# Local attention with normalised probabilities: GpSimd multiplies them by reciprocal sums before TensorE turns them

## The chip, the core and the metric

The kernel runs on one core of one Trainium2 chip, as one program for a whole network. The metric is device time in microseconds (us), the median of the runs. A profiled execution gives a trace of every instruction on the core's engines: TensorE (PE, its weight loads PEld), VectorE (DVE), ScalarE (ACT), GpSimd (POOL) and SyncE (SP), which here only issues transfers.

## The reference

The network has four blocks on 8 sequences of 256 tokens with 128 features. The part that matters here stands in two places: a transformer of six layers whose attention is local. Each layer projects a token row to queries, keys and values of 16 heads of 64, normalises and rotates queries and keys, and attends in windows of 32 tokens, each query to its own window and the one before:

```python
sim = jnp.einsum('bhwie,bhwje->bhwij', bq, bk2) * QK_SCALE
sim = jnp.where(mask, -jnp.finfo(sim.dtype).max, sim)
attn = jax.nn.softmax(sim, -1)
out = jnp.einsum('bhwij,bhwje->bhwie', attn, bv2)
...
out = out.transpose(0, 2, 1, 3).reshape(b, n, INNER)
return out @ Wo
```

A gated feed-forward with a layer norm follows in each layer. The two transformers begin their first full turns at some 641 and 3011 us of the span.

## The kernel before

A turn is one sequence in one layer: 6 layers times 8 sequences are 48 turns for each transformer, 96 in all. The 16 heads of a turn are 8 pairs, and the turn has 8 slots p = 0 to 7, one for a pair. All engines walk through the same slots, each with its own list of calls written out by hand (`pe_window`, `act_window`, `dve_window`, and the loop of GpSimd over `pool_spread` and `pool_prepare`). Engines run in order; semaphores counted up by one tie them together. The lists are skewed: in slot p the scores belong to pair p + 2, and between them lie pieces of the projection and rotation of the next turn (T + 1), and of the feed-forward of the turn two before (T - 2).

A pair goes this way. TensorE makes the scores of pair p + 2 in slot p (`pe_scores`, L1716), two heads in PSUM banks 0 and 1, 128 queries by 128 or 160 keys for the two halves of the sequence. VectorE adds the mask, scales, copies to `pairs` and takes the negated maximum (`dve_negmax`, L2090). ScalarE computes the exponentials in place and their sums (`act_probs`, L1983) a slot later. VectorE takes the reciprocals of the four columns of sums at the start of slot p (`dve_recip`, L2099). TensorE turns the exponentials (four transposes to bank 2, `pe_turn_probs`, L1728 and L1729) first thing in slot p, and ScalarE copies them to `pairsT` (`act_copy_probs`, L1990). VectorE turns the 32x32 blocks of the previous window that the four transposes leave out (`dve_turn_prev`, L2110). In slot p + 1 TensorE multiplies with the values to bank 4 or 5 (`pe_weigh`, L1750).

The division by the sums comes after that product. GpSimd spreads the reciprocals over 64 columns per head (`pool_spread`, L1944), TensorE turns them to the second half of bank 4 or 5 (`pe_shares`, L1738), ScalarE copies this to `shares` (`act_copy_shares`, L1995), and VectorE multiplies context by shares into `ctxT` (`dve_share`, L2104). After all 8 pairs TensorE multiplies by Wo (`pe_out`, L1819), in slot 6 of the next turn.

What else stands in the slots: TensorE makes two projection chunks of the next turn in each of the slots 0 to 5 (`pe_chunks`, L1784) into banks 6 and 7, each of which waits until its bank has been read. ScalarE copies them in the slot behind (`act_copy_chunk`): a query or key chunk needs a square (L2003) and a copy (L2007), a value chunk one copy (L2010), so slots 1, 2, 4 and 5 have four such operations and slots 3 and 6 two. ScalarE's list for a slot begins with these copies. VectorE sums the squares and makes the sine part (`dve_rotate`, L2121 and L2129), GpSimd the cosine part and the sum (L1960, L1967) and scales the keys (L1973). In slots 2 and 6 VectorE works out inverse roots in twelve small steps (`dve_roots`, L2145 to L2151), in slot 2 behind the statistics of the feed-forward (`dve_ff_stats`, L2161 to L2166).

Of the kernel before, what the change touches and what calls it, by code (L numbers as in the profile page):

```python
# [12 lines left out]
ALU = mybir.AluOpType  # L13
# [1613 lines left out]
def windowed_transformers(nc, sem, c, name, io):  # L1627
# [7 lines left out]
             "probs_ready", "probsT_in_psum", "probsT_ready", "prev_ready", "recip_ready", "spread_ready", "ctx_in_psum", "shares_ready", "ctx_ready",  # L1635
# [8 lines left out]
     s.probs_ready, s.probsT_in_psum, s.probsT_ready, s.prev_ready, s.recip_ready, s.spread_ready, s.ctx_in_psum, s.shares_ready, s.ctx_ready,  # L1644
# [51 lines left out]
    def run(number):  # L1696
        T0, T1 = number * TURNS, (number + 1) * TURNS

        def has_turn(turn):
            return T0 <= turn < T1  # L1700
# [20 lines left out]
        def pe_turn_probs(pe, T, p):  # L1721
            pe.wait_ge(s.probs_ready, T * PAIRS + p + 1)
# [9 lines left out]
        def pe_shares(pe, T, p):  # L1732
            pe.wait_ge(s.spread_ready, T * PAIRS + p + 1)
            if T * PAIRS + p - 1 > T0 * PAIRS:

                pe.wait_ge(s.ctx_ready, T * PAIRS + p - 1)
            for t in range(HALVES):
                pe.transpose(c.bank[4 + p % 2][:, S + t * P:S + (t + 1) * P], c.spread[:, p % 2, t * P:(t + 1) * P],  # L1738
                             c.ident[:, :])

        def pe_weigh(pe, T, p):
            pe.wait_ge(s.probsT_ready, T * PAIRS + p + 1)
            pe.wait_ge(s.prev_ready, T * PAIRS + p + 1)
# [143 lines left out]
        def pe_window(pe, T):  # L1887
            following = has_turn(T + 1)
            for p in range(PAIRS):
                pe_turn_probs(pe, T, p)  # L1890
                if p >= 1:
                    pe_shares(pe, T, p - 1)
                elif has_turn(T - 1):
                    pe_shares(pe, T - 1, PAIRS - 1)
# [24 lines left out]
                if p == 5 and has_turn(T - 2):  # L1919
                    pe_turn_normed(pe, T - 2)  # L1920

        def pe_tail(pe):
            L = T1 - 1
            pe_shares(pe, L, PAIRS - 1)
# [14 lines left out]
        def pool_spread(g, T, p):  # L1939
            g.wait_ge(s.recip_ready, T * PAIRS + p + 1)  # L1940
            if T * PAIRS + p - 2 >= T0 * PAIRS:

                g.wait_ge(s.ctx_in_psum, T * PAIRS + p - 1)
            g.tensor_copy(c.spread[:, p % 2, :].rearrange("p (n d) -> p n d", n=4),  # L1944
                          c.recip[:, 0, 4 * (p % 4):4 * (p % 4) + 4].unsqueeze(2).broadcast_to((P, 4, DH))
                          ).then_inc(s.spread_ready, 1)
# [46 lines left out]
        def act_copy_shares(a, T, p):  # L1993
# [531 lines left out]
```

## Time and profile before

| | |
|---|---|
| median of 3 runs | 6058.27 us (6057.07 to 6066.74) |
| the profiled execution: span from first to last instruction | 6062.1 us |
| busy share of the span: PE, DVE, ACT, POOL | 89%, 70%, 65%, 45% |
| one turn in the middle of a transformer | 44.64 us |
| granted TensorE clock, mean over the span | 0.947 |

The profiled execution's own time is its span; it is not timed besides. The busy share counts the time in which an engine runs at least one instruction; matmuls are pipelined, so it is not a share of peak. In the rows below, the order of time on an engine gives the start, the duration, the engine, the line, the operation, its output and inputs and how often it stands there in a row; in brackets stands how long the engine had been idle before it, and what released it. Neighbouring instructions of an engine can overlap in their records by some 0.1 us; the distance between starts is the time that each takes of the queue.

### The profile page before, as it was taken

How to read it: one execution, taken by the hardware profiler on the slowest of the kernel's cores; microseconds unless marked ns; L12 is line 12 of the kernel's file. 1: busy time of each engine (PE TensorE's matmuls, PEld its weight loads, DVE VectorE, ACT ScalarE, POOL GpSimd, SP SyncE). 2: the span in 40 equal slices, each digit the busy share in tenths (PEclk: the TensorE clock that was granted, in tenths of full speed). 3: DMA queues.
4: the chain of work that ended last, by engine and by line, in shares of the span. 5: the costliest groups of instructions: out<-in, count | busy, mean ns of one | idle time of the engine just before them, and what ended most of it. 6: DMA issues, size and time to landing. Idle time of an engine off the chain costs nothing. (4 is left out here: it accounts for less than half of the span.)

```text
span 6062.1 us, 121575 instructions
## 1 busy us (share of the span) xinstructions
PE 5372.5 (89%) x41154; PEld 3794.5 (63%) x41154; DVE 4241.2 (70%) x16112; ACT 3913.4 (65%) x11510; POOL 2700.1 (45%) x2578
## 2 busy tenths in 40 slices
PE   7885699999999999997489999999999999697989
PEld 5674366666666666665256666666666666464678
DVE  4453688888888888885378888788888887454522
ACT  2211588888888888884178888888888888222333
POOL 0000556556565565652166656566565665230000
PEclk9996799999999999998599999999999999697999
DMA  0000000000000000000000000000000000000000
GB/s 11 22 1 3 22 1 12 9 12 9 1 15 6 12 9 12 8 1 4 21 1 7 10 6 12 9 12 9 4 13 6 12 8 1 5 2 4 2 29 8
DMA packets 30964, 53.45 MB, mean 9 GB/s; under 512 B 7688, under 2 KB 17168, under 8 KB 29712
## 3 DMA queue, kind: packets, MB, share of 16 engines
q1 hardware_dynamic: 30352, 45.66, 2.4%
q8 instruction: 339, 5.55, 0.4%
q14 instruction: 273, 2.24, 0.1%
HBM read 44.60 MB, written 1.05 MB: 8 GB/s over the span
## 5 line engine op out<-in xcount | busy, mean ns | idle before, releaser
L1784 PE MATMUL bank<-wA,next_rowT 128*128 128x512 f32 x2304 | 1213.7, 629 | 194.6 <-DVE turnB L2129 73.1
L1983 ACT ACTIVATE pairs<-pairs,negmax 128x128 f32<-128x128 f32 (+1 forms) x3072 | 1236.8, 418 | 18.6 <-DVE negmax L2090 17.5
L1960 POOL TENSOR_TENSOR turnA<-raw,ropes 128x512 f32<-128x512 f32 x768 | 968.7, 1271 | 169.3 <-ACT raw L2007 140.4
L2090 DVE CUSTOM_DVE_ANT_0 pairs<-bank,bands,big 128x128 f32<-128x128 f32 (+1 forms) x3072 | 941.7, 364 | 64.6 <-PE bank L1716 61.0
L1967 POOL TENSOR_TENSOR qk<-turnA,turnB 128x512 f32<-128x512 f32 x768 | 975.8, 1271 | 0.0
L1944 POOL COPY spread<-recip 128x256 f32<-128x256 f32 x768 | 305.3, 398 | 1257.8 <-DVE recip L2099 1251.4
L1784 PEld LDWEIGHTS bank<-wA,next_rowT 128*128 128x128 f32 x2304 | 369.6, 190 | 676.7 <-DVE turnB L2129 294.3
L1990 ACT ACTIVATE pairsT<-bank 128x512 f32<-128x512 f32 x768 | 465.9, 607 | 302.2 <-PE bank L1729 301.9
L1983 ACT ACTIVATION_READ_ACCUMULATOR pairs<-pairs,negmax 128x1 f32 x3072 | 625.0, 203 | 0.0
L285 POOL TENSOR_TENSOR rstd<-vareps,neg_half 128x2 f32<-128x2 f32 x56 | 39.0, 696 | 1292.4 <-DVE vareps L256 892.7
L2129 DVE TENSOR_TENSOR turnB<-bank,ropes 128x512 f32<-128x512 f32 x768 | 523.1, 681 | 0.0
L1973 POOL TENSOR_TENSOR qk<-qk,big 128x1024 f32<-128x1024 f32 x192 | 365.7, 1905 | 341.3 <-DVE recip L2204 327.9
L1807 PE MATMUL bank<-ident,qk 128*128 128x128 f32 x3072 | 431.1, 279 | 41.5 <-ACT big L2010 16.4
L2007 ACT ACTIVATE raw<-bank 128x512 f32<-128x512 f32 x768 | 461.1, 600 | 0.0
L1807 PEld LDWEIGHTS bank<-ident,qk 128*128 128x128 f32 x3072 | 344.7, 142 | 156.1 <-issue 131.6
L1728 PE MATMUL bank<-ident,pairs 128*128 128x128 f32 x1536 | 383.4, 277 | 27.7 <-ACT pairs L1983 27.7
L1729 PE MATMUL bank<-ident,pairs 128*128 128x128 f32 x1536 | 377.7, 273 | 0.0
L1819 PEld LDWEIGHTS bank<-wB,ctxT 128*128 128x128 f32 x3072 | 357.8, 192 | 8.4 <-issue 0.3
L1819 PE MATMUL bank<-wB,ctxT 128*128 128x128 f32 x3072 | 358.8, 275 | 0.0
L1728 PEld LDWEIGHTS bank<-ident,pairs 128*128 128x128 f32 x1536 | 216.1, 141 | 178.3 <-ACT pairs L1983 90.8
L2104 DVE TENSOR_TENSOR ctxT<-bank,shares 128x256 f32<-128x256 f32 x768 | 306.1, 399 | 8.6
L1850 PE MATMUL bank<-xT,wC 128*128 128x256 f32 (+1 forms) x1152 | 305.4, 402 | 6.9 <-ACT big L2038 3.7
(306 smaller groups left out, 11272.8 us busy)
## 6 DMA issues: line engine op xcount, KB each, us to landing
wA<-in_wt_wqkv SPq DMA_DIRECT2D x72, 256.0 KB, 2.8
wB<-in_wt_wo SPq DMA_DIRECT2D x12, 512.0 KB, 3.5
wC<-in_wt_w SPq DMA_DIRECT2D x12, 341.0 KB, 2.9
wD<-in_wt_w SPq DMA_DIRECT2D x12, 192.0 KB, 2.4
big<-in_e_up SPq DMA_DIRECT2D x1, 2048.0 KB
big<-in_e_down SPq DMA_DIRECT2D x1, 2048.0 KB
scl<-in_wt_scales SPq DMA_DIRECT2D x12, 128.0 KB, 3.1
X<-in_x SPq DMA_DIRECT2D x8, 128.0 KB, 2.5
```

The lines of the kernel that those rows point to most:

```text
L1728: pe.transpose(out[:, 0:P], probs[:, 0:P], c.ident[:, :])
L1729: last = pe.transpose(out[:, P:2 * P], probs[:, P + WINDOW:2 * P + WINDOW], c.ident[:, :])
L1784: pe.matmul(side_bank(i)[:, :], c.next_rowT[:, t * P:(t + 1) * P], wqkv[:, k * 512:(k + 1) * 512], start=True, stop=True).then_inc(s.chunk ...
L1807: done = pe.transpose(side_bank(i)[:, (2 * k + t) * P:(2 * k + t + 1) * P], c.qk[:, t, which, at:at + P], c.ident[:, :])
L1819: done = pe.matmul(c.bank[6][:, t * D:(t + 1) * D], ctxT[T % 2][:, k, t * P:(t + 1) * P], wo[:, k * D:(k + 1) * D], start=(k == 0), stop=( ...
L1960: g.tensor_tensor(c.turnA[:, m % 2, :].rearrange("p (h d) -> p h d", h=8), c.raw[:, m % 4, :].rearrange("p (h d) -> p h d", h=8), cos, ALU ...
L1967: g.tensor_tensor(c.qk[:, t, k // 2, (k % 2) * 512:(k % 2) * 512 + 512], c.turnA[:, m % 2, :], c.turnB[:, m % 4, :], ALU.add).then_inc(s.s ...
L1983: last = a.activation(tile, tile, ACT.Exp, scale=-1.0, bias=c.negmax[:, 2 * p + side, t:t + 1], accum_out=c.pair_sums[:, p % 4, t, side:si ...
L1990: a.activation(whole_blocks(c.pairsT[:, 2 * (p % 2):2 * (p % 2) + 2, :]), c.bank[2][:, :].rearrange("p (n k) -> p n k", n=4), ACT.Identity ...
L2007: last = a.activation(c.raw[:, m % 4, :], src, ACT.Identity)
L2090: last = v.tensor_tensor_reduce(c.pairs[:, 2 * (p % 4) + side, AT[t]:AT[t] + SPAN[t]], c.bank[side][:, AT[t]:AT[t] + SPAN[t]], c.bands[:, ...
L2129: v.tensor_tensor(out, turned, sin.unsqueeze(1).broadcast_to((P, 8, 2, DH // 2)), ALU.mult).then_inc(s.chunk_rotated, 1)
```

## The change

The exponentials are multiplied by the reciprocal sums before they are turned, in place in `pairs`, by GpSimd (`pool_shares`, two multiplies for a pair, one for each half). So the product with the values gives the normalised context at once, and ScalarE copies it from PSUM to `ctxT` (`act_copy_ctx`). `pe_shares`, `pool_spread`, `act_copy_shares` and `dve_share` go. `pe_turn_probs` moves from the start to the end of TensorE's slot and waits for GpSimd; `act_copy_probs` moves by one slot, to the same place in the next slot's list; `dve_turn_prev` moves to the end of VectorE's slot and waits for GpSimd too.

```diff
         def pe_turn_probs(pe, T, p):
-            pe.wait_ge(s.probs_ready, T * PAIRS + p + 1)
+            pe.wait_ge(s.shares_ready, T * PAIRS + p + 1)
...
-        def pe_shares(pe, T, p):
-            pe.wait_ge(s.spread_ready, T * PAIRS + p + 1)
-            if T * PAIRS + p - 1 > T0 * PAIRS:
-
-                pe.wait_ge(s.ctx_ready, T * PAIRS + p - 1)
-            for t in range(HALVES):
-                pe.transpose(c.bank[4 + p % 2][:, S + t * P:S + (t + 1) * P], c.spread[:, p % 2, t * P:(t + 1) * P],
-                             c.ident[:, :])
-
         def pe_weigh(pe, T, p):
             pe.wait_ge(s.probsT_ready, T * PAIRS + p + 1)
             pe.wait_ge(s.prev_ready, T * PAIRS + p + 1)
+            if T * PAIRS + p - 1 > T0 * PAIRS:
+
+                pe.wait_ge(s.ctx_ready, T * PAIRS + p - 1)
...
         def pe_window(pe, T):
             following = has_turn(T + 1)
             for p in range(PAIRS):
-                pe_turn_probs(pe, T, p)
-                if p >= 1:
-                    pe_shares(pe, T, p - 1)
-                elif has_turn(T - 1):
-                    pe_shares(pe, T - 1, PAIRS - 1)
                 if p + 2 < PAIRS:
                     pe_scores(pe, T, p + 2)
...
                 if p == 5 and has_turn(T - 2):
                     pe_turn_normed(pe, T - 2)
+                pe_turn_probs(pe, T, p)
...
-        def pool_spread(g, T, p):
+        def pool_shares(g, T, p):
             g.wait_ge(s.recip_ready, T * PAIRS + p + 1)
-            if T * PAIRS + p - 2 >= T0 * PAIRS:
-
-                g.wait_ge(s.ctx_in_psum, T * PAIRS + p - 1)
-            g.tensor_copy(c.spread[:, p % 2, :].rearrange("p (n d) -> p n d", n=4),
-                          c.recip[:, 0, 4 * (p % 4):4 * (p % 4) + 4].unsqueeze(2).broadcast_to((P, 4, DH))
-                          ).then_inc(s.spread_ready, 1)
+            for t in range(HALVES):
+                probs = c.pairs[:, 2 * (p % 4):2 * (p % 4) + 2, AT[t]:AT[t] + SPAN[t]]
+                at = 4 * (p % 4) + 2 * t
+                last = g.tensor_tensor(probs, probs, c.recip[:, 0, at:at + 2].unsqueeze(2).broadcast_to((P, 2, SPAN[t])),
+                                       ALU.mult)
+            last.then_inc(s.shares_ready, 1)
...
-        def act_copy_shares(a, T, p):
+        def act_copy_ctx(a, T, p):
             a.wait_ge(s.ctx_in_psum, T * PAIRS + p + 1)
-            a.activation(c.shares[:, p % 2, :], c.bank[4 + p % 2][:, S:2 * S], ACT.Identity).then_inc(s.shares_ready, 1)
+            a.activation(ctxT[T % 2][:, p, :], c.bank[4 + p % 2][:, 0:S], ACT.Identity).then_inc(s.ctx_ready, 1)
...
-                act_copy_probs(a, T, p)
+                if p >= 1:
+                    act_copy_probs(a, T, p - 1)
+                elif has_turn(T - 1):
+                    act_copy_probs(a, T - 1, PAIRS - 1)
...
-        def dve_share(v, T, p):
+        def dve_turn_prev(v, T, p):
+
             v.wait_ge(s.shares_ready, T * PAIRS + p + 1)
-            v.tensor_tensor(ctxT[T % 2][:, p, :], c.bank[4 + p % 2][:, 0:S], c.shares[:, p % 2, :],
-                            ALU.mult).then_inc(s.ctx_ready, 1)
-
-        def dve_turn_prev(v, T, p):
-
-            v.wait_ge(s.probs_ready, T * PAIRS + p + 1)
+            if T * PAIRS + p - 1 > T0 * PAIRS:
+                v.wait_ge(s.ctx_in_psum, T * PAIRS + p - 1)
...
                 dve_recip(v, T, p)
-                if p >= 2:
-                    dve_share(v, T, p - 2)
-                elif has_turn(T - 1):
-                    dve_share(v, T - 1, p + PAIRS - 2)
-                dve_turn_prev(v, T, p)
                 if p == 7 and has_turn(T - 2):
                     dve_last_hidden(v, T - 2)
...
                     if has_turn(T + 2) and starts_layer(T + 2):
                         dve_tables(v, T + 2)
+                dve_turn_prev(v, T, p)
...
                     for p in range(PAIRS):
-                        pool_spread(g, T, p)
+                        pool_shares(g, T, p)
```

## Rows read from the trace of the kernel before

**Rows 1.** Busy time by stretch (one turn; a later stage), and the next row's transposes.

```profile
2015.03:2059.67 44.64, 42.31 (x305) 29.43 (x303) 36.54 (x146) 36.86 (x113) 26.66 (x26) 1.00 0.13 37
5100.00:5400.00 300.00, 240.60 (x2366) 164.52 (x2366) 156.50 (x501) 103.88 (x262) 97.73 (x46) 0.83 0.01 3
...
L1765 PE MATMUL bank<-ident,Y x192: 272/328/473, 641.2 to 5098.2; 128*128 128x128 f32 x192
```

**Rows 2.** Order of time on TensorE over one turn.

```profile
2015.40 0.71 PE L1750 MATMUL bank<-pairsT,big 128*64 128x160 f32 x8
...
2019.27 0.27 PE L1728 MATMUL bank<-ident,pairs 128*128 128x128 f32 x1
...
2019.70 0.38 PE L1738 MATMUL bank<-ident,spread 128*128 128x128 f32 x2
2020.02 0.77 PE L1716 MATMUL bank<-kT,qT 64*128 64x128 f32 x8
2020.71 0.71 PE L1750 MATMUL bank<-pairsT,V 128*64 128x160 f32 x8
...
2022.80 1.88 PE L1784 MATMUL bank<-wA,next_rowT 128*128 128x512 f32 x4
...
2025.96 0.71 PE L1750 MATMUL bank<-pairsT,V 128*64 128x160 f32 x8
...
2027.76 1.94 PE L1784 MATMUL bank<-wA,next_rowT 128*128 128x512 f32 x4
...
2030.98 0.71 PE L1750 MATMUL bank<-pairsT,V 128*64 128x160 f32 x8
...
2032.96 1.13 PE L1784 MATMUL bank<-wA,next_rowT 128*128 128x512 f32 x2 [0.25 <-ACT qT L2015]
...
2036.89 0.71 PE L1750 MATMUL bank<-pairsT,V 128*64 128x160 f32 x8
...
2041.21 0.71 PE L1750 MATMUL bank<-pairsT,V 128*64 128x160 f32 x8
...
2047.82 0.71 PE L1750 MATMUL bank<-pairsT,V 128*64 128x160 f32 x8
...
2053.86 0.27 PE L1728 MATMUL bank<-ident,pairs 128*128 128x128 f32 x1
...
2055.31 0.71 PE L1750 MATMUL bank<-pairsT,V 128*64 128x160 f32 x8
...
2060.03 0.71 PE L1750 MATMUL bank<-pairsT,V 128*64 128x160 f32 x8
```

**Rows 3.** Order of time on ScalarE, slot 1 and the start of slot 2.

```profile
2019.08 0.58 ACT L2003 ACTIVATE sq<-bank 128x512 f32<-128x512 f32 x1
...
2020.99 0.62 ACT L1990 ACTIVATE pairsT<-bank 128x512 f32<-128x512 f32 x1
...
2023.86 0.60 ACT L2003 ACTIVATE big<-bank 128x512 f32<-128x512 f32 x1 [0.40 <-PE bank L1784]
```

**Rows 4.** Order of time, VectorE and GpSimd in slot 2; all instances of L2166.

```profile
2028.89 1.27 POOL L1967 TENSOR_TENSOR qk<-turnA,turnB 128x512 f32<-128x512 f32 x1
2028.95 1.24 DVE L2166 TENSOR_SCALAR big<-big 128x2 f32<-128x2 f32 x1
...
2030.22 0.18 DVE L2145 TENSOR_SCALAR big<-big 128x34 f32<-128x34 f32 x1
...
2033.04 0.39 DVE L2104 TENSOR_TENSOR ctxT<-bank,shares 128x256 f32<-128x256 f32 x1
...
L2166 DVE TENSOR_SCALAR big<-big x96: 170/1246/1259, 779.2 to 5193.1; 128x2 f32<-128x2 f32 x96
```

**Rows 5.** Groups of instructions by line on GpSimd.

```profile
L1967 POOL TENSOR_TENSOR qk<-turnA,turnB 128x512 f32<-128x512 f32 x768 | 975.8, 1271 | 0.0
...
L1973 POOL TENSOR_TENSOR qk<-qk,big 128x1024 f32<-128x1024 f32 x192 | 365.7, 1905 | 341.3 <-DVE recip L2204 327.9
...
L1944 POOL COPY spread<-recip 128x256 f32<-128x256 f32 x768 | 305.3, 398 | 1257.8 <-DVE recip L2099 1251.4
```

More of the change, by code:

```diff
@@ L1634, in windowed_transformers @@
              "qT_in_psum", "kT_in_psum", "qT_copied", "kT_copied", "scores_ready", "scores_seen", "negmax_ready",
-             "probs_ready", "probsT_in_psum", "probsT_ready", "prev_ready", "recip_ready", "spread_ready", "ctx_in_psum", "shares_ready", "ctx_ready",
+             "probs_ready", "probsT_in_psum", "probsT_ready", "prev_ready", "recip_ready", "shares_ready", "ctx_in_psum", "ctx_ready",
              "out_in_psum", "shifted_in_psum", "normed", "normedT_in_psum", "normedT_ready",
@@ L1643, in windowed_transformers @@
      s.qT_in_psum, s.kT_in_psum, s.qT_copied, s.kT_copied, s.scores_ready, s.scores_seen, s.negmax_ready,
-     s.probs_ready, s.probsT_in_psum, s.probsT_ready, s.prev_ready, s.recip_ready, s.spread_ready, s.ctx_in_psum, s.shares_ready, s.ctx_ready,
+     s.probs_ready, s.probsT_in_psum, s.probsT_ready, s.prev_ready, s.recip_ready, s.shares_ready, s.ctx_in_psum, s.ctx_ready,
      s.out_in_psum, s.shifted_in_psum, s.normed, s.normedT_in_psum, s.normedT_ready,
@@ L1920, in pe_window @@
                     pe_turn_normed(pe, T - 2)
+                pe_turn_probs(pe, T, p)
         def pe_tail(pe):
             L = T1 - 1
-            pe_shares(pe, L, PAIRS - 1)
             pe_weigh(pe, L, PAIRS - 1)
@@ L2062, in act_window @@
                 if p >= 1:
-                    act_copy_shares(a, T, p - 1)
+                    act_copy_ctx(a, T, p - 1)
                 elif has_turn(T - 1):
-                    act_copy_shares(a, T - 1, PAIRS - 1)
+                    act_copy_ctx(a, T - 1, PAIRS - 1)
                 if has_turn(T - 2):
@@ L2073, in act_tail @@
             L = T1 - 1
-            act_copy_shares(a, L, PAIRS - 1)
+            act_copy_probs(a, L, PAIRS - 1)
+            act_copy_ctx(a, L, PAIRS - 1)
             for f in (L - 1, L):
@@ L2256, in dve_tail @@
             L = T1 - 1
-            dve_share(v, L, PAIRS - 2)
-            dve_share(v, L, PAIRS - 1)
             dve_ff_add(v, L - 2)
```

## Prediction

> **What bounds the kernel now.** I read the busy-time view of one turn first [rows 1]. One turn of the local attention takes 44.64 us. TensorE is busy for 42.31 of them, ScalarE for 36.86, VectorE for 36.54 and GpSimd for 26.66, at a granted clock of 1.00. There are 96 such turns in two stages; the transposes of the next row (L1765), two of each turn, run from 641.2 to 5098.2 [rows 1], and 85 of the 94 distances between turns inside a stage lie within 0.02 us of 44.64. So nearly all of both stages is one pattern, and what a turn wins or loses counts some 92 times (the first three turns and the last of each stage differ). The order of time on TensorE [rows 2] then shows a queue with hardly a hole: the eight "weigh" groups of a turn (L1750; I call them W0 to W7 by the slot in which they run) have their successors close behind. TensorE sets the turn, with VectorE just behind it. ScalarE and GpSimd are free enough only as long as nobody waits for them at once. ScalarE's order of time [rows 3] shows how late it is inside a slot: in slot 1 it copies the turned probabilities (L1990) at 2020.99, after four copies of projection chunks and after TensorE has begun the weigh group at 2020.71.
>
> **What the change removes.** Two transposes of the spread sums per slot on TensorE (L1738): from their start to that of the scores 0.32 us pass (2019.70 to 2020.02, [rows 2]); over 768 slots that is at most 246 us. By the pitch of the four transposes before them (0.43 us for four, 2019.27 to 2019.70) it is at least 165 us. On VectorE a product of 0.39 us per slot goes (L2104, [rows 4]). On ScalarE one 128x256 copy takes another's place and costs nothing new. On GpSimd a copy of 398 ns goes [rows 5].
>
> **What it adds.** Two in-place GpSimd multiplies per slot, of 256 and 320 elements a partition. No row has this shape. The nearest is L1973, in place with a broadcast factor as here: 1905 ns for 1024 elements [rows 5]. In proportion 576 elements are 1.07 us: the low end. A line through it and L1967 (1271 ns for 512) has 0.64 us fixed per instruction and gives 0.95 + 1.03 = 1.99 us: the high end. L1967's own rate, 2.48 ns an element, gives 1.43. I take 1.4 us, 1.0 us more than the copy that goes, since it lies between the two. GpSimd's turn becomes 26.7 + 8.0 = 34.7 us, which is no bound by its sum; it would be one from some 2.9 us a pair on.
>
> **What it moves.** Three things that were half a slot or more early now sit on a loop. (a) The probabilities of a pair are turned at the slot's end, their ScalarE copy comes a slot later, behind the chunk copies, and the weigh group stands only the scores (0.69 us, 2020.02 to 2020.71) behind the transposes. (b) VectorE's turn of the previous window's part (L2110) goes to the very end of its slot. In slot 2 that is behind the feed-forward statistics and the inverse roots, and the weigh group of slot 3 waits for it. (c) The transposes wait for GpSimd. Behind a waiting weigh group stands all of TensorE's later work, the next chunks first, and behind these stand ScalarE's copies and VectorE's rotations.
>
> **The new turn, worked out.** Zero is the start of W0, at 2015.40. Before, W1 to W7 and the next W0 start at 5.31, 10.56, 15.58, 21.49, 25.81, 32.42, 39.91 and 44.63 [rows 2].
>
> W1: ScalarE starts the chunk copies at 3.68 as before (2019.08, [rows 3]); four copies take 1.91 (to 2020.99), the probabilities' copy 0.62 and the semaphore 0.07: 6.28. TensorE, its scores done at 5.0, waits 1.3 us.
>
> W2: W1 to the next chunks is 2.09 (2020.71 to 2022.80, [rows 2]), from there to ScalarE's first copy 1.06 (2023.86, [rows 3]), then 1.91 + 0.62 + 0.07: 12.03.
>
> W3: W2 to the end of the shift is 1.80 (2025.96 to 2027.76, [rows 2]) and 0.15 to VectorE; the statistics start at 13.98 and take 0.8, so L2166 is ready at 14.8. Here [rows 4] count: on 128x2 elements L2166 took 1.24 us and ended within 0.03 us of the GpSimd addition (L1967) beside it. So did nearly all of its 96 instances (median 1246 ns, shortest 170). GpSimd's queue is later now by its multiply: from 9.3, 1.4 + four operations at 1.25 = 15.7. The roots start behind it at 15.95 and take 2.73 (2030.22 to 2033.04, less 0.09 for a reciprocal), the turn and the semaphore 0.35: W3 at 19.05, 3.5 us later than before. This is the largest single term.
>
> The Trainium skill, page "SBUF — State Buffer", section "Who interferes with whom", says that VectorE and GpSimd share a port pair which one instruction holds to its end while the other blocks fully; the trace agrees at this operation. By it the turn is the one worked out here; with no blocking W3 would be 0.9 us earlier and the turn some 45.4 us.
>
> W4: W3 to the chunks is 1.98 (2030.98 to 2032.96, [rows 2]; the late query and key blocks), then 1.06 + 1.91 + 0.62 + 0.07 = 5.64: 24.7. VectorE's wait before the second chunk of this slot goes.
>
> W5: ScalarE is now never idle from one probabilities' copy to the next: copy, exponentials and context copy 2.47 (2020.99 to 2023.86, less the 0.40 that it idled), four chunk copies 1.91: 4.38, so 29.1 [rows 3].
>
> W6: from W5 0.64 to the first chunk, 0.90 to the second, 1.06 to ScalarE, 0.60 its value copy, 0.8 for the last turns: transposes at +4.0. Behind them 0.64 to ScalarE, 0.60 its copy, 0.07: +5.3, so 34.4. Some 1.0 us of waits and slow chunks of before go here.
>
> W7: W6 to the transposes is 6.04 as before (2047.82 to 2053.86, [rows 2]), then 1.31 for the ScalarE copy: 41.75. The roots and L2110 of slot 6 lie under the 6.04.
>
> W0: W7 to the transposes 2.65; then VectorE copies the keys (0.6), makes the first hidden products (0.85) and only then turns: +1.9. The next W0 is at 46.3.
>
> The turn goes from 44.63 to 46.3 us: +1.7 us, over 92 turns +156 us. Prologue and tail change by less than 5 us. The profiled execution spans 6062.1 us, 4 us above the median of 6058.27; so 6062 + 156 - 4, some 6215 us. If GpSimd's pair costs 1.99 us, W3 moves 0.6 later: +55 us, 6270. If it costs 1.07, GpSimd is done 0.3 earlier: -30 us, 6185. Eight joints, each good to 0.1 us, make 0.7 us a turn or 65 us. The forecast's own range is 6130 to 6320.
>
> **Rivals.** *The queues have the slack, and only the removed transposes count.* For it: TensorE is busy 95% of a turn, and what is removed lies on it. If every new wait stays under other work, the gain is 165 to 246 us: 5812 to 5893. Against: W1's wait needs only ScalarE's order, which [rows 3] show. It decides where the copy of L1990 lands against the scores: up to 0.7 us behind the transposes it is hidden. If half of the waits that I count were hidden, the turn would end near or below the old one. 10% for faster. *Gain and waits cancel:* 4%, within 0.2%, about what a measurement of this kernel can tell from no change. *Only ScalarE's loop counts,* L2110 not being late (roots unblocked, statistics early): W3 at 17 to 18, a turn of 44.9 to 45.4, 6080 to 6130: 12%. *GpSimd becomes the bound or is blocked.* Its multiply and VectorE's roots meet in slot 6, from 35 on. If each instruction there blocks the other's next, the roots end up to 2.6 us later and the key scaling at some 42, its use being at 44; with 2.9 us a pair or more the turn would be 47.5 and longer: 6320 to 6450, 8%. *The clock falls.* A stretch with TensorE busy at 80% has a granted clock of 0.83 [rows 1]; in the new turn TensorE is at some 87%, with a hole of 2.5 us ahead of W3. A few hundredths lost make it 6300 to 6450. Against: nearly all of what fills the other 13% are holes below 1.5 us. 4%. The forecast has the remaining 62%.
>
> **Range.** 6080 to 6340 leaves out faster and same (14%) and some 6% above. Chances: faster 0.10, within 0.2% 0.04, slower 0.86.
>
> **What would show it.** Right: no L1738 rows; L1750 preceded by waits for L1990 in slots 1, 2, 4 and 5 of 0.6 to 1.3 us each, and for L2110 in slot 3 of about 2.5 us; a turn of 46.3 us; GpSimd multiplies of some 0.6 and 0.75 us; TensorE's busy share of a turn down to some 87%; the clock at 1.00. Wrong if the wait ahead of W1 is under 0.3 us (then ScalarE's copies were not in the way), if L2110 is not what W3 waits for, or if the multiplies take over 1 us each.

## The result

| | us | against before, 95% interval |
|---|---|---|
| before, median | 6057.70 (6057.07 to 6066.74) | |
| after, median | 6373.98 (6367.06 to 6375.07) | 1.0516 [1.0503, 1.0530] |
| after, the profiled execution's span | 6373.3 | |
| forecast | 6215 (6080 to 6340) | 1.026 |

The change costs 316 us, twice the 157 us forecast. The page of the kernel after: busy time by engine, and the granted TensorE clock in 40 slices.

```profile
PE 5250.6 (82%) x39618; PEld 3720.6 (58%) x39618; DVE 4091.5 (64%) x15344; ACT 3908.1 (61%) x11510; POOL 3374.2 (53%) x3346
...
PEclk9995899999999999998589999999999999787999
```

TensorE, busy 89% of the span before, is at 82%. Next the busy time of two successive turns of the kernel after, and of three pieces of the second (columns: length; busy time and instructions of PE, PEld, DVE, ACT, POOL; granted clock; DMA).

```profile
2211.70:2258.74 47.04, 40.03 (x288) 27.89 (x287) 35.32 (x139) 36.77 (x113) 33.71 (x35) 1.00 0.04 13
2258.74:2306.98 48.24, 41.49 (x288) 28.97 (x287) 34.70 (x139) 36.77 (x113) 33.76 (x35) 0.96 0.03 8
...
2263.00:2277.00 14.00, 10.87 (x80) 7.32 (x78) 11.88 (x43) 10.65 (x34) 10.76 (x11) 1.00 0.00 1
2277.00:2283.00 6.00, 5.12 (x21) 3.35 (x22) 2.91 (x16) 2.41 (x8) 4.42 (x4) 0.72 0.00 1
2283.00:2306.98 23.98, 21.58 (x166) 15.80 (x164) 17.66 (x71) 19.96 (x58) 16.95 (x18) 1.00 0.06 16
```

A turn takes 44.64 us in [rows 1]; now 47.04, and TensorE's busy share of it is 40.03 / 47.04 = 85%. The second turn does the same work in 48.24, and all of the difference lies in its piece from 2277 to 2283, with a granted clock of 0.72. Turns are measured from one start of L1759 to the next (the next row's transposes, L1765 before). From the fifth turn of a stage on, about one turn in three (30 of 86) takes 47.02 to 47.05 us, and the others 48.09 to 48.54. With the fourth turn of each stage, that is over 88 turns, the mean is 47.80.

The order of time on TensorE through the undisturbed turn, the one that keeps its full clock:

```profile
2210.63 0.77 PE L1716 MATMUL bank<-kT,qT 64*128 64x128 f32 x8 [0.68 <-ACT qT L2004]
...
2211.70 0.71 PE L1744 MATMUL bank<-pairsT,big 128*64 128x160 f32 x8
...
2217.96 0.71 PE L1744 MATMUL bank<-pairsT,V 128*64 128x160 f32 x8 [1.10 <-ACT pairsT L1979]
...
2223.71 0.71 PE L1744 MATMUL bank<-pairsT,V 128*64 128x160 f32 x8 [0.65 <-ACT pairsT L1979]
...
2230.85 0.71 PE L1744 MATMUL bank<-pairsT,V 128*64 128x160 f32 x8 [2.27 <-issue]
...
2236.61 0.71 PE L1744 MATMUL bank<-pairsT,V 128*64 128x160 f32 x8 [0.65 <-ACT pairsT L1979]
...
2241.02 0.71 PE L1744 MATMUL bank<-pairsT,V 128*64 128x160 f32 x8 [0.66 <-ACT pairsT L1979]
...
2246.57 0.71 PE L1744 MATMUL bank<-pairsT,V 128*64 128x160 f32 x8
...
2253.91 0.71 PE L1744 MATMUL bank<-pairsT,V 128*64 128x160 f32 x8
...
2257.67 0.77 PE L1716 MATMUL bank<-big 64*128 64x128 f32 x8 [0.68 <-ACT big L2004]
2258.74 0.71 PE L1744 MATMUL bank<-pairsT,V 128*64 128x160 f32 x8
```

The weigh groups (L1744) are W0 to W7 and the next W0. Where [rows 2] have none, W1, W2, W4 and W5 now stand behind waits for ScalarE's copy (L1979), and W3 behind one of 2.27 us. The profile names no releaser there; VectorE's and GpSimd's orders of time in slot 2 do:

```profile
2226.34 1.27 POOL L1956 TENSOR_TENSOR qk<-turnA,turnB 128x512 f32<-128x512 f32 x1
...
2226.53 1.11 DVE L2156 TENSOR_SCALAR big<-big 128x2 f32<-128x2 f32 x1
2227.67 0.18 DVE L2135 TENSOR_SCALAR big<-big 128x34 f32<-128x34 f32 x1
...
2230.51 0.24 DVE L2100 STREAM_TRANSPOSE pairsT<-pairs 32x64 f32<-32x64 f32 x1
```

VectorE's last step of the slot, the turn of the previous window, ends at 2230.75, and W3 starts 0.10 later. The blocked step of [rows 4] is there again (1.11 us; it ends at 2227.64 beside the addition's 2227.61). Then the multiplies, among GpSimd's groups by line (busy, mean ns):

```profile
L1933 POOL TENSOR_TENSOR pairs<-pairs,recip 128x320 f32<-128x320 f32 x768 | 552.9, 720 | 0.0
...
L1933 POOL TENSOR_TENSOR pairs<-pairs,recip 128x256 f32<-128x256 f32 x768 | 470.8, 613 | 1071.8 <-DVE recip L2092 1071.5
```

One zero for all, the start of W0, in the undisturbed turn:

| | W1 | W2 | W3 | W4 | W5 | W6 | W7 | W0 |
|---|---|---|---|---|---|---|---|---|
| before | 5.31 | 10.56 | 15.58 | 21.49 | 25.81 | 32.42 | 39.91 | 44.63 |
| forecast | 6.28 | 12.03 | 19.05 | 24.7 | 29.1 | 34.4 | 41.75 | 46.3 |
| after | 6.26 | 12.01 | 19.15 | 24.91 | 29.32 | 34.87 | 42.21 | 47.04 |

The first three joints are right to 0.1 us. Some 0.6 us are lost in the later ones, and 0.8 more by the clock in the mean turn. The experiments had to say what each is, and why the removed work gave so little back.

### The profile page after: what moved, and what is told of

Same layout as the page of the kernel before. It is cut to its first block and busy times, and to the rows that moved or that the text cites. A ratio compares the mean times of both kernels' runs of the same rounds, so it can differ in the third digit from the quotient of the medians.

```text
span 6373.3 us, 117819 instructions
## 1 busy us (share of the span) xinstructions
PE 5250.6 (82%) x39618; PEld 3720.6 (58%) x39618; DVE 4091.5 (64%) x15344; ACT 3908.1 (61%) x11510; POOL 3374.2 (53%) x3346
## 3 DMA queue, kind: packets, MB, share of 16 engines
q8 instruction: 324, 5.31, 0.3%
## 5 line engine op out<-in xcount | busy, mean ns | idle before, releaser
L1933 POOL TENSOR_TENSOR pairs<-pairs,recip 128x256 f32<-128x256 f32 (+1 forms) x1536 | 991.3, 666 | 1071.8 <-DVE recip L2092 1071.5
L1778 PE MATMUL bank<-wA,next_rowT 128*128 128x512 f32 x2304 | 1159.2, 626 | 64.7 <-ACT qT L2004 21.2
L1778 PEld LDWEIGHTS bank<-wA,next_rowT 128*128 128x128 f32 x2304 | 402.8, 197 | 445.4 <-issue 302.0
L1979 ACT ACTIVATE pairsT<-bank 128x512 f32<-128x512 f32 x768 | 468.4, 610 | 298.4 <-PE bank L1729 298.4
L1801 PE MATMUL bank<-ident,qk 128*128 128x128 f32 x3072 | 487.2, 303 | 31.1 <-ACT V L1999 11.2
L1744 PE MATMUL bank<-pairsT,big 128*64 128x160 f32 (+1 forms) x3072 | 290.2, 312 | 257.4 <-ACT pairsT L1979 148.4
L1744 PE MATMUL bank<-pairsT,V 128*64 128x160 f32 (+1 forms) x3072 | 284.1, 307 | 264.3 <-ACT pairsT L1979 145.6
L1801 PEld LDWEIGHTS bank<-ident,qk 128*128 128x128 f32 x3072 | 380.5, 155 | 172.4 <-issue 158.8
L1744 PEld LDWEIGHTS bank<-pairsT,V 128*64 128x64 f32 x3072 | 189.0, 140 | 349.0 <-ACT pairsT L1979 210.7
L1744 PEld LDWEIGHTS bank<-pairsT,big 128*64 128x64 f32 x3072 | 193.0, 142 | 342.1 <-ACT pairsT L1979 214.0
```

The source lines that it names most:

```text
L1744: last = pe.matmul(out[DH * side:DH * side + DH, q0:q1], V[T % 2][:, kt, 2 * p + side, :], c.pairsT[:, 2 * (p % 2) + side, at:at + q1 - q0 ...
L1778: pe.matmul(side_bank(i)[:, :], c.next_rowT[:, t * P:(t + 1) * P], wqkv[:, k * 512:(k + 1) * 512], start=True, stop=True).then_inc(s.chunk ...
L1801: done = pe.transpose(side_bank(i)[:, (2 * k + t) * P:(2 * k + t + 1) * P], c.qk[:, t, which, at:at + P], c.ident[:, :])
L1933: last = g.tensor_tensor(probs, probs, c.recip[:, 0, at:at + 2].unsqueeze(2).broadcast_to((P, 2, SPAN[t])), ALU.mult)
L1979: a.activation(whole_blocks(c.pairsT[:, 2 * (p % 2):2 * (p % 2) + 2, :]), c.bank[2][:, :].rearrange("p (n k) -> p n k", n=4), ACT.Identity ...
```

## Experiments: where the loss sits

My theory was that the loss is the sum of two late loops, ScalarE's copy of the turned probabilities and VectorE's turn of the previous window, with the clock on top. The rivals were GpSimd's price, and a loss of cover elsewhere.

**The turn of the previous window early.** The kernel after, but in slot 2 this step runs ahead of the feed-forward statistics and the roots:

```diff
+                if p == 2:
+                    dve_turn_prev(v, T, p)
                 if p == 2 and has_turn(T - 2):
                     dve_ff_stats(v, T - 2)
...
-                dve_turn_prev(v, T, p)
+                if p != 2:
+                    dve_turn_prev(v, T, p)
```

> The changed kernel, with VectorE's turn of the previous window's part (L2100) of slot 2 put back ahead of the feed-forward statistics and the roots; all else as changed. Theory (the hole ahead of the weigh group of slot 3 comes from this place in VectorE's queue, and the clock falls because of this hole): W3 comes some 2.2 us earlier, the hole falls under 0.3 us, the granted clock stays at 1.00 in every turn, the turn is 44.8 us in place of a mean of 47.9, the kernel some 6085 us. Rival (ScalarE's late copies set W3 anyway): turn 47 us or more, 6290 us. Rival (the clock falls because TensorE is less busy in all, not because of the hole): clock still 0.96 to 0.97 per turn, turn 45.7, 6170 us.

Measured: 6097.53 us, ratio 1.0063 [1.0046, 1.0079], a turn of 44.81 us (every eighth 45.17). The waits for ScalarE's copy stay (1.10, 0.65, 0.65, 0.65), the hole ahead of W3 goes, and so do the slow stretches: the mean clock of the span is back from 0.931 to 0.947. One step in one slot of eight holds 276 of the 316 us.

**The hole filled.** The kernel after with 18 transposes to an unused half bank ahead of W3; their product isn't used.

```diff
+                if p == 3:
+                    for n in range(18):
+                        pe.transpose(c.bank[4][:, S:S + P], c.ident[:, :], c.ident[:, :])
                 if p >= 1:
                     pe_weigh(pe, T, p - 1)
```

> The changed kernel, with 18 transposes of the identity to the unused half of bank 4 put on TensorE between the scores and the weigh group of slot 3: 2.0 us of work in a hole of 2.3 us, nothing else changed; what they write is read by nobody. Theory (the hole makes the granted clock fall, and the fall costs 1.2 us in two of three turns): every turn is 47.04 us at a clock of 1.00, the kernel some 6290 us, 80 us less than the changed kernel. Rival (the clock falls for another reason, or its fall costs nothing on the path): 6370 us or more.

Measured: 6307.99 us, 1.0408 [1.0393, 1.0424]. Busy time of one turn, and the order of time on TensorE at the place:

```profile
1994.99:2042.03 47.04, 42.14 (x306) 29.84 (x305) 35.27 (x139) 36.76 (x113) 33.72 (x34) 1.00 0.00 1
...
2012.17 2.18 PE L1892 MATMUL bank<-ident 128*128 128x128 f32 x18
...
2014.52 0.71 PE L1744 MATMUL bank<-pairsT,V 128*64 128x160 f32 x8 [0.16 <-issue]
```

The filler hurries nothing: the turn is the undisturbed turn of the kernel after. But now every turn is one of those (47.02 to 47.05, every eighth 47.40). So 66 us of the 316 are the clock's; an idle stretch costs more than its length here.

The filler raises TensorE's busy share as well as closing the hole, so this run alone doesn't say which of the two the clock answers to. Two runs of the next sections do. The same 1000 us of each, first with VectorE's turn late alone (a hole of 2.20 us a turn), then the kernel called "all early, GpSimd later" below (its longest hole is 1.74 us):

```profile
1500.00:2500.00 1000.00, 921.65 (x6512) 650.96 (x6511) 786.50 (x3137) 788.72 (x2428) 573.10 (x556) 0.98 0.03 9
```

```profile
1500.00:2500.00 1000.00, 893.68 (x6324) 604.91 (x6322) 800.11 (x3050) 820.58 (x2501) 743.83 (x752) 1.00 0.03 9
```

The busier one, at 92% (91% in a turn at full clock), loses clock (0.98), and the one at 89% keeps 1.00. The kernel called "all early" is busy 89% too (892.84 us), with holes of 1.5 and 1.8 us a turn, and has 0.98. So the busy share of a turn is not what decides; the slower clock goes with the long holes.

**The moves alone, and each by itself.** The kernel before, with its spread sums, shares and product, and (first) all three moves, (second) the transposes where they were and VectorE's turn at the slot's end, (third) the transposes at the slot's end with ScalarE's copy a slot later, and VectorE's turn where it was.

```diff
@@ first and third, TensorE and ScalarE
-                pe_turn_probs(pe, T, p)
                 if p >= 1:
                     pe_shares(pe, T, p - 1)
...
+                pe_turn_probs(pe, T, p)
...
-                act_copy_probs(a, T, p)
+                if p >= 1:
+                    act_copy_probs(a, T, p - 1)
+                elif has_turn(T - 1):
+                    act_copy_probs(a, T - 1, PAIRS - 1)
@@ first and second, VectorE
-                dve_turn_prev(v, T, p)
                 if p == 7 and has_turn(T - 2):
...
+                dve_turn_prev(v, T, p)
```

> The kernel before with its own normalisation (spread, transposes, product), and only the three moves of the change: the transposes of probabilities at the end of TensorE's slot, their ScalarE copy a slot later, VectorE's turn of the previous window's part at the end of its slot. No GpSimd multiply. Theory (the loss comes from the places in the queues, not from GpSimd's price): a turn of 47.0 to 48.5 us, the same hole of about 2 us ahead of W3, 6290 to 6430 us. Rival (waiting for GpSimd's multiply is the cost): a turn near 45 us, under 6130 us.

> The kernel before with one move alone: VectorE's turn of the previous window's part at the end of its slot. Theory (in slot 2 it then stands behind the roots, and the weigh group of slot 3 waits for it): a hole of 2 us or more ahead of that group, the clock under 1.00 in part of the turns, turn 45.6 to 47.0 us, 6150 to 6290 us. Rival (without the late copies VectorE's queue is early enough): under 6090 us.

> The kernel before with the other move alone: the transposes of the probabilities at the end of TensorE's slot and their ScalarE copy a slot later, VectorE's turn where it was. Theory (holes ahead of the weigh groups of slots 1, 2, 4 and 5 of 0.4 to 1.1 us, since the transposes of the sums still stand before the scores): clock 1.00, turn 45.2 to 46.2 us, 6110 to 6210 us. Rival (together with the other move it costs less than each alone would sum to, because the same wait is hit twice): 6100 us or less.

Measured: 6351.59 us, 1.0485 [1.0469, 1.0500] for all; 6244.03, 1.0307 [1.0291, 1.0322] for VectorE's turn late alone; 6139.67, 1.0134 [1.0117, 1.0151] for the transposes late alone. The weigh groups that wait longest in the second and the third:

```profile
1998.52 0.71 PE L1750 MATMUL bank<-pairsT,V 128*64 128x160 f32 x8 [2.20 <-DVE pairsT L2110]
```

```profile
1999.29 0.71 PE L1750 MATMUL bank<-pairsT,big 128*64 128x160 f32 x8 [0.89 <-ACT pairsT L1990]
```

The moves without the new arithmetic cost 294 us (6351.59 - 6057.70); the parts are 186 and 82 and add to 268, so 26 us come only with both. The last 22 us, from 294 to 316, are GpSimd's multiplies together with all that the change removes: the removed work gives back nothing that can be seen while the loops are late. The next run, with the multiplies cut nearly to nothing, says the same: 6357.42 us can't be told from the 6351.59 of the moves alone.

## Experiments: GpSimd's price, and what the removed work is worth

**Small multiplies.** The kernel after, each multiply only on the first 8 columns of its block: all other probabilities stay unnormalised.

```diff
-                probs = c.pairs[:, 2 * (p % 4):2 * (p % 4) + 2, AT[t]:AT[t] + SPAN[t]]
+                probs = c.pairs[:, 2 * (p % 4):2 * (p % 4) + 2, AT[t]:AT[t] + 8]
...
```

> The changed kernel with the GpSimd multiplies cut to 8 columns of each tile (16 elements in place of 256 and 320); it leaves out nearly all of the division by the sums. Queues and waits as changed. It measures GpSimd's price alone. Theory (the queues' places make the loss, GpSimd's time enters only through VectorE's blocked step in slot 2): W3 comes 0.5 to 1 us earlier, turn 46.0 to 46.6 us, kernel 6190 to 6270 us. Rival (GpSimd's multiply is half of the loss or more): turn under 45.8 us, under 6170 us.

Measured: 6357.42 us, 1.0491 [1.0473, 1.0508], far above both ranges. The pair takes 0.39 us in place of some 1.3, W3 still waits 2.06 us, and the turns run from 46.82 to 48.38. VectorE and GpSimd in slot 2:

```profile
1977.18 0.39 POOL L1933 TENSOR_TENSOR pairs<-pairs,recip 128x16 f32<-128x16 f32 x2 [0.98 <-DVE recip L2092]
1978.23 1.27 POOL L1949 TENSOR_TENSOR turnA<-raw,ropes 128x512 f32<-128x512 f32 x1 [0.66 <-ACT raw L1996]
...
1982.10 1.27 POOL L1956 TENSOR_TENSOR qk<-turnA,turnB 128x512 f32<-128x512 f32 x1
1982.49 0.90 DVE L2156 TENSOR_SCALAR big<-big 128x2 f32<-128x2 f32 x1
```

GpSimd is done with the pair 0.9 us sooner and then waits 0.66 us for ScalarE's copy of a chunk, so its last addition ends only 0.20 us earlier in the turn and still blocks VectorE's step. A cheaper multiply is worth 17 us in all. What a dearer one would have cost, no run tried.

**The normalisation left out.** The kernel before with its order, without spread sums, shares and product; the context stays undivided, and ScalarE copies it straight from PSUM.

```diff
-                    pe_shares(pe, T, p - 1)
...
-                        pool_spread(g, T, p)
...
-                    dve_share(v, T, p - 2)
...
-            a.activation(c.shares[:, p % 2, :], c.bank[4 + p % 2][:, S:2 * S], ACT.Identity).then_inc(s.shares_ready, 1)
+            a.activation(ctxT[T % 2][:, p, :], c.bank[4 + p % 2][:, 0:S], ACT.Identity).then_inc(s.ctx_ready, 1)
```

> The kernel before, in its own order, without the normalisation: no spread, no transposes of it, no product; ScalarE copies the context as it is. It leaves out the division by the sums. It measures what the removed work is worth alone. By the pitch of the transposes (0.22 to 0.32 us a slot): turn 42.1 to 42.9 us, kernel 5812 to 5893 us. Rival (TensorE's place is taken by ScalarE or VectorE at once): turn 43.8 us or more, 5980 us or more.

Measured: 6024.85 us, 0.9941 [0.9926, 0.9956], a turn of 44.24. So the gain is 33 us, and not 165 to 246. VectorE's order of time in slot 2:

```profile
2018.27 0.17 DVE L2165 TENSOR_SCALAR big<-big 128x2 f32<-128x2 f32 x1
2018.47 1.17 DVE L2144 TENSOR_SCALAR big<-big 128x34 f32<-128x34 f32 x1
2019.67 1.20 DVE L2145 TENSOR_SCALAR ints<-big 128x34 int32<-128x34 int32 x1
2020.91 0.18 DVE L2146 TENSOR_SCALAR newton<-ints 128x34 int32<-128x34 int32 x1
```

The step that was blocked before (now L2165) is free, and two others stretch in its stead. The key copies wait behind these, and TensorE waits for a key copy before its second chunk in slot 3:

```profile
2024.42 1.13 PE L1786 MATMUL bank<-wA,next_rowT 128*128 128x512 f32 x2 [1.33 <-DVE kT L2114]
```

What TensorE gains is waited away there.

**The same with GpSimd elsewhere.** First two of GpSimd's operations (`cos3` and `add2`) were written into slot 3. This changed nothing: without the spread copies GpSimd has no wait at a slot's start and runs through the same sequence as its data come. Then only `add2` was put there, together with a wait for the roots at the start of slot 3. Last came the same order without that wait, on the full kernel before, whose spread copies tie GpSimd to the slots. The edits of these last two:

```diff
-POOL_SLOTS = {1: ("cos0", "cos1", "add0"), 2: ("cos2", "add1", "cos3", "add2"), 3: ("add3", "scale0"),
+POOL_SLOTS = {1: ("cos0", "cos1", "add0"), 2: ("cos2", "add1", "cos3"), 3: ("add2", "add3", "scale0"),
@@ the kernel without the normalisation alone, pool_prepare
+                if slot == 3:
+                    g.wait_ge(s.rs_ready, q * 2 + 1)
```

> The kernel of e3_no_norm (before, without the normalisation) with two of GpSimd's operations of slot 2 (cos3, add2) put into slot 3, so that GpSimd is idle while VectorE makes its statistics and roots; the division is left out as there. Theory (the gain of the removed transposes was lost because three of VectorE's small steps in slot 2 stood blocked beside GpSimd's operations, 2.4 us where they take 0.5): these steps take 0.18 us each, the wait of 1.33 us before the second chunk of slot 3 goes, turn 43.0 to 43.6 us, kernel 5910 to 5970 us. Rival (VectorE or ScalarE holds the turn at 44.2 anyway, or GpSimd is late for the sums of slot 3): turn 44.0 us or more.

> The kernel of e3_no_norm with GpSimd's addition add2 in slot 3 and a wait of GpSimd for VectorE's roots ahead of slot 3's additions, so that this time it really is idle beside them (in e7_no_norm_pool_late nothing held it back). The division is left out. Theory (the gain of the removed transposes went into VectorE's blocked steps in slot 2): L2144 and L2145 take 0.2 us each, the wait of 1.33 us in slot 3 goes, turn 42.8 to 43.4 us, 5890 to 5945 us. Rival: turn 44.0 or more, the gain is held elsewhere.

> The kernel before with one edit: GpSimd's addition add2 moves from slot 2 to the front of slot 3. Theory (the 1.24 us that L2166 takes beside GpSimd's addition is on the path through the key copy of slot 3, by at most the 0.39 us that TensorE waits there): turn 44.2 to 44.5 us, 6020 to 6045 us. Rival (off the path): 6058 us within 0.2%.

Measured, in this order: 6024.68 us, 0.9943 [0.9928, 0.9957] without the wait, a missed expectation; 5839.16, 0.9637 [0.9624, 0.9650] and a turn of 42.31 with it, better than expected; and 5968.94, 0.9848 [0.9835, 0.9862], a turn of 43.65, for the full kernel with one addition moved, more than twice the gain that was expected. All instances of the blocked step in the last:

```profile
L2166 DVE TENSOR_SCALAR big<-big x96: 168/169/313, 777.0 to 5108.1; 128x2 f32<-128x2 f32 x96
```

The median is 169 ns, against 1246 in [rows 4]. The Trainium skill, page "SBUF — State Buffer", section "Who interferes with whom", has VectorE share one of its two port pairs with GpSimd: where VectorE's instruction uses both, whoever issues first holds the shared pair for the whole instruction, and the other blocks. This pair of runs agrees: the step is 1.08 us shorter with no GpSimd instruction beside it, and the turn is 0.99 us shorter.

From 6057.70 to 5839.16 are some 218 us, but 89 of them come from GpSimd's order alone, with nothing removed. So the removed work is worth 33 us by itself and some 130 us (5968.94 to 5839.16) once GpSimd is out of VectorE's way.

## Experiments: can the change pay?

If what is late is the order alone, an early order should win. Built on the first experiment:

| kernel | edit | us | ratio |
|---|---|---|---|
| all early | transposes ahead of the chunks in slots 0, 1, 2 and 4 and ahead of the output product in 6, ScalarE's copy first in slots 1, 2, 3 and 5 | 6191.68 | 1.0219 [1.0204, 1.0234] |
| the same, VectorE's turn late | as above without the first experiment's edit | 6367.46 | 1.0509 [1.0493, 1.0525] |
| all early, GpSimd later | all early, `add2` to slot 3, key scaling ahead of the rest in slot 4 | 6141.73 | 1.0134 [1.0121, 1.0148] |
| GpSimd later alone | the first experiment with that GpSimd order | 6095.83 | 1.0060 [1.0046, 1.0073] |
| first slots early | transposes early in slots 0 to 2 only, copy first in slots 1 to 3, that GpSimd order | 5998.09 | 0.9903 [0.9888, 0.9917] |

The edit of the last, on TensorE and ScalarE. The others differ in the sets of slots, and those called all early also have the transposes of slot 6 ahead of the output product:

```diff
+                if p in (0, 1, 2):
+                    pe_turn_probs(pe, T, p)
                 if following:
                     pe_prepare(pe, T + 1, p, False)
...
-                pe_turn_probs(pe, T, p)
+                if p >= 3:
+                    pe_turn_probs(pe, T, p)
...
+                if p in (1, 2, 3):
+                    act_copy_probs(a, T, p - 1)
                 if following:
                     for i in ACT_CHUNK_SLOTS.get(p, ()):
...
-                if p >= 1:
+                if p >= 4:
                     act_copy_probs(a, T, p - 1)
```

> The kernel of e1_prev_early, with TensorE's transposes of the probabilities ahead of the projection chunks in slots 0, 1, 2 and 4 and ahead of the product with Wo in slot 6, and their ScalarE copy ahead of the chunk copies in slots 1, 2, 3 and 5. Theory (what is left of the loss is ScalarE's copy landing behind the chunk copies): the holes of 0.65 and 1.1 us ahead of the weigh groups of slots 1, 2 and 5 close, the turn falls from 44.81 us under 44.2 and the kernel under the one before, some 5960 to 6030 us. Rival (ScalarE and VectorE are at their own limit in slots 1 to 5, the waits only move): turn 44.5 to 44.9, 6050 to 6100 us.

> The kernel of e5_early_turn with VectorE's turn of slot 2 back at the end of its slot, behind the roots, as in the changed kernel. Theory (that place alone costs a hole of 2 us or more ahead of the weigh group of slot 3, and the clock with it): turn 46 to 47 us, clock under 1.00 in part of the turns, 6190 to 6290 us. Rival (with the other waits gone VectorE's queue has the slack for it): within 30 us of e5_early_turn.

> The kernel of e5_early_turn, with two GpSimd operations put later in its list: the addition add2 from slot 2 to slot 3 (behind the multiply that waits for VectorE's roots) and the key scaling scale0 from slot 3 to the front of slot 4 behind that slot's multiply. Theory (what made e5_early_turn slow is two holes: 1.5 us in slot 3, made by VectorE's small steps standing blocked beside add2, and 1.8 us in slot 4, made by the multiply standing behind scale0): both holes fall under 0.6 us, the clock stays at 1.00, turn 43.2 to 44.2 us, kernel 5930 to 6020 us, faster than the kernel before. Rival (ScalarE holds slots 1 to 5 at about its own sum): turn 44.4 us or more, 6040 us or more.

> The kernel of e1_prev_early with the GpSimd order of e9_early_pool_order, transposes and ScalarE copies left where the change put them. Theory: VectorE's blocked steps were hidden there by the wait for ScalarE, so little changes: turn 44.3 to 44.8 us, 6040 to 6097 us; the difference to e9_early_pool_order is what the place of the transposes and their copies costs. Rival: under 44.0 us, that place costs nothing.

> The kernel of e9_early_pool_order, with the transposes and their ScalarE copy early only in slots 0 to 2 (copies in slots 1 to 3), and where the change put them in slots 3 to 7. Theory (in e9_early_pool_order slots 1 to 3 gained 2.4 us, and TensorE's waits for the GpSimd multiply in slots 4 and 6, 1.0 and 1.7 us, ate them): these two waits go, turn 42.6 to 43.3 us, kernel 5870 to 5935 us, faster than before and than e10_before_pool_order. Rival (ScalarE and VectorE then hold it): turn 44 us or more, 6000 us or more.

Only the fourth came within its expectation. The first three and the last were slower than their theories said: the first lies above even its rival's range, the second above its own, the third in its rival's, and the last 2 us short of its rival's. Chunks and transposes of the first in slots 3 and 4:

```profile
2123.24 1.10 PE L1778 MATMUL bank<-wA,next_rowT 128*128 128x512 f32 x2 [1.54 <-DVE big L2112]
...
2128.47 0.33 PE L1728 MATMUL bank<-ident,pairs 128*128 128x128 f32 x1 [1.75 <-POOL pairs L1938]
```

Early transposes reach GpSimd before it is done: in slot 4 they wait 1.75 us for the multiplies, with the chunks behind them, and in slot 3 VectorE's blocked steps hold the chunk. Its turns run from 45.15 to 47.10. With VectorE's turn late as well, nothing is left of the gain over the kernel after. With GpSimd's addition and key scaling later the kernel takes 45.18 a turn and waits 1.00 and 1.74 us for GpSimd in slots 4 and 6. GpSimd's order on top of the first experiment alone changes nothing that can be told (6095.83 against 6097.53). Only where the transposes go early just in slots 0 to 2, where GpSimd has the time, does the kernel beat the one before, by 60 us; seven of eight of its turns take 43.65, and waits for ScalarE's copy of 0.53, 0.65 and 0.56 us stay. But the kernel before with GpSimd's one addition moved is 29 us faster still. So an order was found in which the new normalisation beats the kernel as it was, and none in which it beats the old normalisation with GpSimd's order mended.

## Why the prediction was wrong

The direction held, for the reasons given, and the size did not. Three steps failed: the clock, taken at 1.00 in the sum; W6 and above all W0, which wait for something other than the forecast says; and the turns and stretches outside the steady pattern, put at under 5 us. In the prediction's own steps:

**W1 and W2** (6.28 and 12.03) were measured at 6.26 and 12.01, with waits of 1.10 and 0.65 us for ScalarE's copy. The forecast had 0.6 to 1.3 us for slots 1, 2, 4 and 5. Alone this loop, with the late transposes in all slots, costs 82 us.

**W3** (19.05) came at 19.15. The blocked step, the roots behind it and the turn at the slot's end were right one by one; the wait is 2.27 us where about 2.5 were named. The experiment that takes this step forward makes it the largest single term, as forecast, and with the clock it is 276 us.

**W4 to W6** (24.7, 29.1 and 34.4) came at 24.91, 29.32 and 34.87: the first and the last were mis-sized, by 0.11 and 0.25 us beyond what the joint before had. W6 was forecast behind ScalarE's copy of the probabilities, 5.3 us after W5. The rows have it 5.55 us after W5, behind the scores, and these start 0.10 us after the end of VectorE's key copy, which `pe_scores` waits for:

```profile
2245.09 0.69 DVE L2105 COPY big<-bank 128x512 f32<-128x512 f32 x1 [1.74 <-PE bank L1801]
2245.88 0.77 PE L1716 MATMUL bank<-big 64*128 64x128 f32 x8 [0.18 <-issue]
```

**W7** kept its distance to W6 (7.34 us, forecast 7.35).

**W0** was mis-sized by 0.28 us: its step was forecast as 4.55 (46.3 less 41.75) and measured as 4.83. The forecast lets it wait for VectorE's turn of the previous window, 1.9 us behind the transposes. That turn is on time and is not what W0 waits for:

```profile
2258.09 0.24 DVE L2100 STREAM_TRANSPOSE pairsT<-pairs 32x64 f32<-32x64 f32 x1
```

It ends 1.94 us behind the transposes' start at 2256.39, and W0 starts 0.41 us after it, behind the late scores. The step went wrong where the prediction removes work from TensorE's path and never asks who waits under it. The kernel before at the start of slot 0, on ScalarE and TensorE:

```profile
2058.28 0.58 ACT L2015 ACTIVATE big<-bank 128x512 f32<-128x512 f32 x1
```

```profile
2058.17 0.33 PE L1728 MATMUL bank<-ident,pairs 128*128 128x128 f32 x1 [0.21 <-ACT pairs L1983]
...
2058.97 0.77 PE L1716 MATMUL bank<-big 64*128 64x128 f32 x8
```

ScalarE's copy of the next queries comes out under 0.80 us of transposes (2058.17 to 2058.97), and the scores find it done. Now the scores stand first in slot 0, and they wait 0.68 us for the same copy (L2004; twice in the rows of the result). Both gates, of W6 and of W0, are read from the rows; no run put other work in their place.

**The clock** was a rival at 4%, for 6300 to 6450 us, and it came about, though the measured time lies in its range only together with the other misses: the clock makes 66 of the 159 us that the forecast lacks, and the mean over the span fell by 0.016 (0.947 to 0.931), not by the few hundredths named. The reason against it, that nearly all holes are below 1.5 us, overlooked that the one hole above it, which the forecast itself had at 2.5 us, can be enough. It costs 47.80 - 47.04 = 0.76 us a turn; the kernel with the filled hole has a mean of 47.05 over the same 88 turns.

**The number of turns.** The forecast took 92 turns of one kind and under 5 us for the rest. By the starts of the turns the two stages have 88 steady turns; the first three of each are others, and they lose 11 and 10 us (135.6 against 124.4 in the first stage, 133.6 against 123.8 in the second). What lies outside the two stretches of turns loses 11 us.

The whole of the 311 us between the two profiled spans is then: 88 x 1.66 = 146 as forecast, 88 x 0.74 = 65 for the joints from W3 on, 88 x 0.76 = 67 for the clock (the filled hole: 66), 21 in the first three turns and 11 outside. That makes 310.

**GpSimd's pair** was taken at 1.4 us with ends of 1.07 and 1.99. The records give 0.613 + 0.720 = 1.33, and no multiply took over 1 us. The effect of the low end (30 us for 0.3 us less) was too large: 0.9 us less gave 17 us, since GpSimd then waits for ScalarE's copy, and W3 for the roots all the same (2.06 us). The effect of the high end, 55 us, was not tried.

**The first rival**, that only the removed transposes count and 165 to 246 us are gained, fell twice. The waits for ScalarE's copy are there, and the removal alone gives 33 us. The 130 us that it can give need GpSimd held back, which the change doesn't do. *Only ScalarE's loop counts* (6080 to 6130) is, as a kernel, the first experiment: 6097.53.

## What to carry to other kernels

A step moved to the end of an engine's list costs what stands between, and the work taken from the front of another engine's list was someone's cover: for each removal, ask what was waiting behind it unseen. Price the hole and not only the time: one hole of 2.27 us in a pattern that repeats took the clock along here, so that a step worth some 2 us a turn cost more than its length. Where VectorE runs a chain of tiny steps that others wait for, try GpSimd's long operations elsewhere before changing any arithmetic. Here that was the best edit of all that keep the division, 89 us for one moved addition on the kernel before; on the first experiment's kernel, where TensorE waits for ScalarE instead, the like order gave nothing.

## What the runs showed of the hardware

One hole in a turn can bring the granted clock down. In a turn with TensorE busy 85% of the time, a hole of 2.27 us is followed, in two turns of three, by a stretch at the lower of its two levels (1.2 of 2.4 GHz), while the third turn, with the same hole and busy share, keeps 1.00. What singles that turn out is not shown. The rows right behind the hole of the second turn above:

```profile
2277.89 1.03 PE L1744 MATMUL bank<-pairsT,big 128*64 128x160 f32 x8 [2.26 <-issue]
2278.85 1.97 PE L1801 MATMUL bank<-ident,qk 128*128 128x128 f32 x8
2280.65 2.41 PE L1778 MATMUL bank<-wA,next_rowT 128*128 128x512 f32 x4
```

The weigh group takes 1.03 us where it took 0.71, and the eight matmuls behind it (L1801) 1.97 where they took 1.09. About every third turn is spared through both stages, and a fill that does no work of use buys the clock back. A shorter hole is not always milder: with the small multiplies it is 2.06 us, and only 13 of 86 turns keep the full clock, against 30. The first experiment's turn has nine waits of 0.18 to 1.10 us and a busy share of 40.19 / 44.81 = 90%, and its clock is 1.00. VectorE's turn late alone, with one hole of 2.20 us, has a busy share of 92% over 1000 us and a clock of 0.98.

Even VectorE's smallest steps last until GpSimd's instruction beside them ends: 128x2 and 128x34 elements take 0.17 to 0.18 us alone and 1.11 to 1.24 beside a 1.27 us addition, six to seven times as long. In the kernel without normalisation two such steps in a row were blocked, by two successive GpSimd instructions.
